# One program stretch for phase A, and a different order of its by-products

## The reference, cut to what matters

```python
x = x + jnp.tanh(g_xattn[0]) * _L0_xattn_ref(ctx_1024, _layernorm(x), mask, ...)   # 16 heads of 64, 512 keys
x = x + jnp.tanh(g_ffn[0]) * _L0_ffn_ref(_layernorm(x), ...)                       # 16 heads of 16, gated
x = x + jnp.tanh(g_xattn[1]) * _L1_xattn_ref(_layernorm(x), ctx_1024, ..., 16)     # 16 heads of 16
x = x + jnp.tanh(g_ffn[1]) * _L1_ffn_ref(_layernorm(x), ...)                       # 32 experts, best 1
...   # layers 2 and 3: an attention, a small net, an attention, 32 experts with the best 4
```

## Time and profile before

| what | us |
|---|---|
| median of 3 runs | 4738.97 (4735.92 to 4742.37) |
| profiled execution, own time | 4746.18 |
| its span | 4744.5 |
| PE busy | 4112.5 (87%) |
| DVE busy | 2320.8 (49%) |
| ACT busy | 1780.9 (38%) |
| POOL busy | 953.1 (20%) |

### The profile page before, as it was taken

How to read it: one execution, slowest core, us unless ns; L and a number is a source line. 1 busy time by engine, 2 the same in 40 slices (tenths; PEclk the granted TensorE clock), 3 DMA queues, 4 the chain that set the end, 5 groups by cost and what they waited for, 6 DMA issues and landing times. The chain is left out here.

```text
span 4744.5 us, 77442 instructions
## 1 busy us (share of the span) xinstructions
PE 4112.5 (87%) x29168; PEld 2852.5 (60%) x29168; DVE 2320.8 (49%) x7126; ACT 1780.9 (38%) x3733; POOL 953.1 (20%) x1113
## 2 busy tenths in 40 slices
PE   5999899989998999999996699996899899769986
PEld 3655655565556555655564359995566666438853
DVE  2545554555455545554543322212556666574335
ACT  3445444544554455445542111111343444313320
POOL 1212221222122212221211001111000010005557
PEclk9999999999999999999997799996899999879998
DMA  3000000000000000000000207991000000028974
GB/s 104 1 3 8 8 3 5 8 8 3 6 8 8 3 6 8 8 3 6 6 5 5 107 5 245 333 325 58 12 21 23 19 21 15 12 85 317 389 202 125
DMA packets 132637, 300.85 MB, mean 63 GB/s; under 512 B 19953, under 2 KB 86065, under 8 KB 123697
## 3 DMA queue, kind: packets, MB, share of 16 engines
q1 hardware_dynamic: 81968, 216.69, 12.8%
q0 software_dynamic: 18336, 50.09, 3.7%
q10 hardware_dynamic: 31968, 29.11, 1.8%
HBM read 245.76 MB, written 50.07 MB: 62 GB/s over the span
## 5 line engine op out<-in xcount | busy, mean ns | idle before, releaser
L487 POOL TENSOR_SCALAR a_wide_p<-a_wide_p,a_w_inv 128x512 f32<-128x512 f32 x512 | 362.7, 721 | 1553.1 <-DVE a_w_inv L1029 1552.1
L851 ACT ACTIVATE a_wide_p<-a_wide_p,a_row_min 128x512 f32<-128x512 f32 x512 | 364.1, 713 | 46.7 <-DVE a_row_min L1024 42.3
L1099 DVE TENSOR_REDUCE a_q_pad<-ring 128x4 f32<-128x1024 f32 x256 | 301.7, 1221 | 155.5 <-PE ring L679 151.7
L1024 DVE CUSTOM_DVE_ANT_0 a_wide_p<-ring,a_neg_keys 128x512 f32<-128x512 f32 x434 | 285.0, 687 | 108.9 <-PE ring L553 108.1
L553 PE MATMUL ring<-a_qk 64*128 64x512 f32 x868 | 291.7, 647 | 3.7 <-DVE a_wide_pt L1034 1.6
L899 ACT ACTIVATE a_probs<-ring 128x1024 f32<-128x1024 f32 x256 | 247.4, 1019 | 90.0 <-PE ring L693 90.0
L1446 PE MATMUL ring<-b_xgt,b_we 128*128 128x128 f32 x2016 | 235.9, 275 | 2.8 <-issue 2.3
L1446 PEld LDWEIGHTS ring<-b_xgt,b_we 128*128 128x128 f32 x2016 | 230.1, 192 | 4.1 <-issue 3.2
L2418 DVE CUSTOM_DVE_ANT_0 c_junk<-ring,c_neg_mask 128x256 f32<-128x256 f32 x512 | 182.6, 420 | 99.7 <-PE ring L1985 99.2
L583 PE MATMUL ring<-a_wide_pt,a_v 128*64 128x256 f32 x1792 | 219.8, 388 | 0.0
L679 PE MATMUL ring<-a_k_t,a_q_t 32*128 32x256 f32 x2048 | 154.2, 415 | 73.4 <-DVE a_q_pad L1099 48.9
(11 more groups left out here) (429 smaller groups left out, 8362.6 us busy)
## 6 DMA issues: line engine op xcount, KB each, us to landing
b_we<-in_experts SPq DMA_DIRECT2D x63, 1536.0 KB, 9.6
d_we<-in_experts SPq DMA_DIRECT2D x159, 384.0 KB, 6.2
d_results<-d_yb ACTq DMA_DIRECT2D x159, 128.0 KB, 6.1
b_results<-b_yb ACTq DMA_DIRECT2D x63, 128.0 KB, 9.3
x_all<-in_x SPq DMA_DIRECT2D x1, 4096.0 KB, 14.1
a_cb<-in_ctx SPq DMA_DIRECT2D x16, 256.0 KB, 2.7
b_turned<-a_heads_t SPq DMA_DIRECT2D x16, 256.0 KB, 2.4
b_rows<-a_heads SPq DMA_DIRECT2D x16, 256.0 KB, 2.1
```

The source lines that it names most:

```text
L487: ins = pool.tensor_scalar(wide_p[:, h % 4, t, :], wide_p[:, h % 4, t, :], w_inv[:, t, h:h + 1], 1.0, ALU.mult, ALU.mult)
L851: ins = act.activation(wide_p[:, h % 4, t, :], wide_p[:, h % 4, t, :], ACT.Exp, scale=-1.0, bias=row_min[:, h, t:t + 1], accum_out=row_sum ...
L1024: dve.tensor_tensor_reduce(wide_p[:, h % 4, t, :], wbank(name), neg_keys[w % 2][:], -0.125, 3.0e38, ALU.add, ALU.min, row_min[:, h, t:t + ...
L1099: dve.tensor_reduce(q_pad[:, :, 2 * i:2 * i + 2, HD].rearrange("p t h -> p h t"), s, AX.X, ALU.max, negate=True).then_inc(nr.taken(name), 1)
```

## The change

The two stretches ahead of the main one are gone, and their work stands at the head of the main one. SP issues, in this order: the first context, the first two tiles of `x`, `wkv`, `wq`, the mask, the two other contexts, the rest of `x`, and then the 21 remaining loads. ACT issues the temperature, the gates and the four norm columns. Each group has a semaphore of its own, on which its first reader waits. DVE waits for the remaining loads in `constants()`, ahead of step 2 of round 0.

In the loop, six things stand elsewhere:

- DVE's reciprocal of the second tile's sums, in steps 1, 4 and 6, stands ahead of the norms at the third place of the step, and POOL scales that tile ahead of two roots.
- In step 7, PE transposes the first tile of weights, and DVE copies it, ahead of a group by query and of its maxima.
- The fourth group by query stands later: that of f after the scores of t=1 in step 4, that of c in step 0 of the next round, after the first scores. The maxima follow.
- The counting of the routing moves from place 22 to 23, DVE's ranking after the l norm.
- ACT copies f's turned queries ahead of the exponentials of the second tile in step 3.
- ACT's narrow exponentials of one group stand between the two copies of weights, and its first copy of the summed values stands one place earlier, before the next wide exponentials.

```diff
-        with Stage() as ctx:
...
-                sp.dma_start(x_all[:], a["x"].rearrange("b (t p) d -> p (b t) d", p=P)).then_inc(loaded, 16)
-                sp.dma_start(gates[:, 0:4], every("g_xattn")).then_inc(loaded, 16)
-                sp.dma_start(gates[:, 4:8], every("g_ffn")).then_inc(loaded, 16)
-                sp.wait_ge(loaded, 48)
...
-                act.wait_ge(loaded, 48)
-                act.activation(gates[:], gates[:], ACT.Tanh).then_inc(gated, 1)
...
-                with Stage() as ctx:
...
-                    loads = [
-                        (wq[:], a["L0_xattn_Wq"].rearrange("(c p) n -> p c n", p=P)),
-                        (wkv[:], a["L0_xattn_Wkv"].rearrange("(c p) n -> p c n", p=P)),
-                        (wout[:], a["L0_xattn_Wout"].rearrange("(c p) n -> p c n", p=P)),
...
-                        (temp[:, 0, :], every("temperature_row")),
-                        (w1[:], a["w1_t"].rearrange("(c p) n -> p c n", p=P)),
...
-                    @block.sync
-                    def _(sp):
-                        for dst, src in loads:
-                            sp.dma_start(dst, src).then_inc(loaded, 16)
-                        sp.wait_ge(loaded, 16 * len(loads))
...
-                        dve.wait_ge(loaded, 16 * len(loads))
...
+                    loads = [
+                        (wout[:], a["L0_xattn_Wout"].rearrange("(c p) n -> p c n", p=P)),
+                        (ln_o[:, 0, :], every("L0_xattn_ln_o_g")), (ln_o[:, 1, :], every("L0_xattn_ln_o_b")),
...
+                        x = a["x"].rearrange("b (t p) d -> p (b t) d", p=P)
+                        context(0)
+                        sp.dma_start(x_all[:, 0:2, :], x[:, 0:2, :]).then_inc(first_loaded, 16)
+                        sp.dma_start(wkv[:], a["L0_xattn_Wkv"].rearrange("(c p) n -> p c n", p=P)).then_inc(wkv_loaded, 16)
+                        sp.dma_start(wq[:], a["L0_xattn_Wq"].rearrange("(c p) n -> p c n", p=P)).then_inc(wq_loaded, 16)
+                        sp.dma_start(mask_u8[:], every("mask_keys")).then_inc(mask_loaded, 16)
+                        for b in range(1, min(B, 3)):
                             context(b)
+                        sp.dma_start(x_all[:, 2:T, :], x[:, 2:T, :]).then_inc(latents_loaded, 16)
+                        for dst, src in loads:
+                            sp.dma_start(dst, src).then_inc(loaded, 16)
...
-                                if u == 1 and on(f):
-                                    root("o", o_norm, f + 1)
-                                if u == 6 and on(f):
-                                    root("c", c_norm, f + 1)
                                 if on(i):
                                     scale(i, u, 1)
                                 if u == 1 and on(f):
+                                    root("o", o_norm, f + 1)
                                     root("f", f_norm, f + 1)
+                                if u == 6 and on(f):
+                                    root("c", c_norm, f + 1)
...
                                     e_logits(c0)
-                                if p == 22:
+                                if p == 23:
                                     e_count(c0)
...
                                     queries("f", f)
-                                if 17 <= p <= 20:
+                                if 17 <= p <= 19:
                                     by_query("f", f, p - 17)
...
                                     queries("c", f)
-                                if 36 <= p <= 39:
+                                if 36 <= p <= 38:
                                     by_query("c", f, p - 36)
...
+                        pe.wait_ge(made, 2)
                         for i in range(-1, B + 2):
+                            if i == 1:
+                                pe.wait_ge(loaded, 16 * len(loads))
+                                pe.wait_ge(made, 10)
                             for u in range(PAIRS):
                                 nw, nu = pair_after(i, u)
                                 bw, bu = pair_before(i, u)
                                 if on(i):
                                     scores(i, u, 0)
+                                if u == 0 and on(i - 2):
+                                    by_query("c", i - 2, 3)
                                 if on(nw):
                                     keys(nw, nu)
                                 beside(i, 5 * u)
                                 if on(i):
                                     scores(i, u, 1)
+                                if u == 4 and on(i - 1):
+                                    by_query("f", i - 1, 3)
                                 if on(nw):
                                     pair_queries(nw, nu)
                                 beside(i, 5 * u + 1)
@@ -825,9 +784,12 @@
                                 beside(i, 5 * u + 2)
                                 if on(bw):
                                     pair_values(bw, bu)
+                                if u == PAIRS - 1 and on(i):
+                                    weights_by_key(i, u, 0)
                                 beside(i, 5 * u + 3)
+                                if u < PAIRS - 1 and on(i):
+                                    weights_by_key(i, u, 0)
                                 if on(i):
-                                    weights_by_key(i, u, 0)
                                     weights_by_key(i, u, 1)
                                 beside(i, 5 * u + 4)
...
-                                if p in (5, 6):
-                                    values_out("c", c0, p - 5)
-                                if 2 <= p <= 5:
-                                    narrow_exps("c", c0, p - 2)
+                                if p in (2, 4, 5):
+                                    narrow_exps("c", c0, (2 * p - 4, 2 * p - 3))
+                                if p in (4, 6):
+                                    values_out("c", c0, p // 2 - 2)
...
-                                if p == 16:
-                                    turn_queries(("f", "Q", f))
                                 if p == 22:
                                     nr.wait_full(act, ("f", "S", f, 7))
                                     turn_queries(("f", "Q2", f))
-                                if p in (26, 27):
-                                    values_out("f", f, p - 26)
-                                if 23 <= p <= 26:
-                                    narrow_exps("f", f, p - 23)
+                                if 24 <= p <= 26:
+                                    narrow_exps("f", f, (2 * p - 46, 2 * p - 45))
+                                if p in (25, 27):
+                                    values_out("f", f, (p - 25) // 2)
...
+                        act.dma_start(temp[:, 0, :], every("temperature_row")).then_inc(temp_loaded, 16)
+                        act.dma_start(gates[:, 0:4], every("g_xattn")).then_inc(gates_loaded, 16)
+                        act.dma_start(gates[:, 4:8], every("g_ffn")).then_inc(gates_loaded, 16)
+                        for i, n in enumerate(("ln_x_g_cols", "ln_x_b_cols", "ln_l_g_cols", "ln_l_b_cols")):
+                            act.dma_start(ln_cols[:, i, :], a[n]).then_inc(ln_loaded, 16)
+                        act.wait_ge(gates_loaded, 32)
+                        act.activation(gates[:], gates[:], ACT.Tanh).then_inc(gated, 1)
+                        act.wait_ge(stepped, 1)
+                        act.activation(temp[:, 2, :], temp[:, 1, :], ACT.Exp).then_inc(stepped, 1)
+                        act.wait_ge(stepped, 3)
+                        act.activation(temp[:, 4, :], temp[:, 3, :], ACT.Ln).then_inc(stepped, 1)
+                        act.wait_ge(ln_loaded, 64)
...
+                                if u == 3 and on(i - 1):
+                                    turn_queries(("f", "Q", i - 1))
...
-                                if on(i):
-                                    take_weights(i, u, 0)
-                                    take_weights(i, u, 1)
+                                for t in range(2):
+                                    if u == 0 and on(i - 2):
+                                        narrow_exps("c", i - 2, (2 + t,))
+                                    if u == 4 and on(i - 1):
+                                        narrow_exps("f", i - 1, (t,))
+                                    if on(i):
+                                        take_weights(i, u, t)
                                 beside(i, 5 * u + 4)
...
+                                if p == 0:
+                                    maxima("c", c0, 3)
...
-                                if 17 <= p <= 20:
+                                if 17 <= p <= 19:
                                     maxima("f", f, p - 17)
+                                if p == 21:
+                                    maxima("f", f, 3)
...
+                        def constants():
```

(19 more changed lines are left out.)

156 lines of the change are left out of this document (76 added, 80 removed).

## The result

| kernel | median us | runs |
|---|---|---|
| before | 4737.44 (4729.70 to 4742.37) | 4 |
| after | 4538.99 (4537.02 to 4539.24) | 4 |

The ratio is 0.9576, 95% interval 0.9562 to 0.9589: 198.5 us less. The forecast was 168.3 us less, 4570.7 us. The time lies in the wide range, 4530 to 4620, but outside the inner one of 4548 to 4600, and it is nearer to the rival "more than forecast" (4524 us) than to the forecast itself. The profiled execution of after took 4539.24 us, its span is 4537.5, against 4744.5 before: 207.0 us.

The account below looks back on a forecast made before the run. Loads and waits for them bound the opening, PE the loop. Opening 36.9, rounds 2 to 15 123.2, round 1 6.0 and round 16 2.2 sum to 168.3 us off 4738.97: 4570.7 us, range 4530 to 4620, inner 4548 to 4600.

Parts of the forecast that it names:

- more than forecast: Rival: in the rounds the waits vanish with little behind them, 12 us a round; 4524 us, chance 0.08.
- The opening: Before the loop: first scores 38.7 us earlier once the mask row's loads land at 14.9; less 1.8 for constants, 36.9 us.
- The gates: In the opening: at best landed in 3 us at no cost, at worst at 15.6, costing 7.2 us; the first was taken.
- Step 1: In a round: POOL's wait of 1.74 us goes, the rest turns into a wait for DVE; gain 0.4 us.
- the named wait for DVE's copy: Sign: PE's scores of step 2 wait for DVE's copy of weights, once a round, over 1 us.
- The walk of the full round: Gains at each wait of a full round, summing to 9.4 us; 8.8 after a deduction, a round of 148.7.
- steps 3 to 5: In a round, with f's attention: five waits go, sum 5.7 us, 0.6 let come back; gain 5.1 us.
- step 6: In a round: POOL's scaling wait of 1.74 us goes, ACT's copies follow PE by 0.2; gain 1.5 us.
- the further deduction of 0.6 for hops: Taken off the round's 9.4 us for engine-to-engine latency left out where a wait nearly closes; leaves 8.8 us.
- c's part: Step 7 to step 1, c's attention: group and row-minimum waits 1.0 us, earlier copy of summed values 1.42; gain 2.4 us.
- the other terms: Outside the 13 full rounds: opening 36.9 us, first interval 6.0, last interval 8.8, last mark to end 2.2.
- the 147 to 151 named as a sign: Sign in the loop: the wide output product should recur every 147 to 151 us in the changed kernel's profile.

Follow-up runs that it names:

- e1: before without its two opening stretches, with the loads of after (old loop behind new opening): 4703.8 us, 0.9925 of before.
- e8: after with the mask loaded ahead of wkv, norm columns ahead of the gates on ACT's queue, DVE's wait for ACT's exponential behind the first norms: 4542.4 us.
- e6: after with step 7's transposes and copy of the first tile of weights behind the wide output again: 4557.0 us.
- e10: before with only DVE's reciprocal ahead of the norms in steps 1, 4 and 6 and POOL's scaling ahead of its roots: 4697.4 us.
- e3: after with DVE's second-tile reciprocal behind the norms again in steps 1, 4 and 6, POOL's roots ahead of its scaling: 4582.8 us.
- e11: after with SP loading norm columns and mask ahead of wkv, DVE's wait for ACT's exponential behind first norms, ln_o's bias added in step 0: 4522.85 us.

## Why the prediction was right, and where it was short

*The opening*: right in its chain, 38.5 by the marks, 37.1 by e1, for 36.9. What ended the chain is the one named, the mask row, at 16.17 us instead of 14.9. The norm columns, which the working didn't price, were there at 15.8, 1.3 us ahead of the latents' transposes. The first scores start at 24.86 for 24.2, a gain of 38.0 instead of 38.7. `constants()` stood at 47.59 us without a wait, between 45 and 50, and made PE wait for 0.67 us (at 50.96) where 1.8 were taken off; there are 18 loads behind it, not 21, and they were there by 40.5 us instead of 43.8. The size is in part luck: in before the granted clock is 0.55 from 72.7 to 76.5 us, in step 0, in after 1.00 at that place, which is 1.2 us that the forecast knew nothing of.

*The gates*: priced at no cost by choice, with 7.2 us as the other bound. No row stood behind the 3 us of the lower bound; here they took 3.9 and 5.2 us and landed at 5.1 and 6.9 us, which costs nothing, as DVE then stood for 3.45 us for the mask. The rule of the Trainium skill that the prediction cites, "DMA: Bandwidth & Descriptors", section on queues, rings and completion order, has the transfer engines take turns between queues. The gates agree with it; the columns issued from 2.2 us on do so only in part, as 1 KB took 8.8 to 11.8 us beside SP's stream. e8 shows that the other bound was real: gates of 2 KB behind four small transfers came at 15.9 us, where the bound had 15.6. So the choice was right by luck: it hung on the gates standing ahead of the columns in ACT's queue, which the prediction had not used as an argument.

*Step 1*: the mechanism is right, and the named wait for DVE's copy stands there with 0.92 us, for "over 1 us". DVE's work from c's heads to the copy is 5.96 us instead of 6.77. The gain is 0.83 for 0.4, as DVE's and POOL's contention went too (0.72 us of DVE's time).

*The walk of the full round* gave 9.4, and 10.60 was measured against the round that was walked. It had 11.6 us of waits that go and 2.1 that come back (1.3 in step 1, 0.6 in steps 3 to 5, 0.2 in step 6). In the two traces 12.5 us of PE's waits go and 2.3 come back: 0.92 for DVE's copy, and 0.3 each for ACT's `a_kv_t` in step 6, for its copy of weights where the row minimum stood, and twice for exponentials. So what came back was already in the walk, and the further deduction of 0.6 for hops was the first step that failed. The second lies in *c's part*, 2.94 for 2.4: of its three waits for maxima, 0.55, 0.65 and 0.60 us, only one of 0.55 is left, where the walk took 0.2 off the last alone. The row for the maxima is the one that the earlier trace rows leaves out; the 15.6 us of idle time are not all in its six rows. That e6's edit carries half of c's gain, 1.46 us a round, the forecast did not see; it priced the group's move as if the copy of weights stayed early by itself.

*Half clock* is the third, by omission: 0.77 us a round, and with the longer idle time of the other rounds 1.05. The working took one round of 157.51 us, the second shortest, for all. The range of intervals, 157.5 to 159.6, was there to be read, and e10 shows that the sums' edit alone ends it.

In sum: 13 full rounds gave 150.8 - 114.4 = 36.4 us more than forecast; the other terms together 2.3. By the medians the shortfall is 30.2, as 8.5 us of the 207.0 are the profiled executions' own. The rounds, of 146.9 us, lie just under the 147 to 151 named as a sign, and they gained nearly the 12 us of the rival "more than forecast". As it has it, the waits vanish with little behind them (12.5 us against 2.3); 0.77 of the 11.6 us is the clock, which it doesn't name.

## What to carry to other kernels

Read more than one round, and compare their lengths before taking one for all: where a loop does the same work each time and its rounds have two lengths, the difference is not in its list; here it was mostly the clock behind a wait. Where an edit moves work away from in front of an instruction, look at every bank that this instruction needs: a copy that was early enough becomes late, and the edit that repairs it costs 3 us when tried in the old order and is worth 20 us beside the other. And where an engine works without a gap before a wait, changing the order renames the wait; taking something out of the stretch shortens it.

## What the runs showed that was not expected

- A product of 1.89 us took up to 3.55 (clock 0.52) behind a wait of 1.99 us for POOL, in 5 of the 13 full rounds of before and again in e1 and e3; once in before the fall came behind a wait of 1.60. In the eleven kernels where these waits are gone, no full round is longer by such a step.
- DVE's two-input operations took 689 and 632 ns beside POOL's scaling, and 480 and 482 without it; in e3, where they meet again, one group has 808 on average.
- Transfers of 1 and 2 KB from ACT's queue landed 3.5 to 5.2 us after their issue when issued by 1.8 us, and 7.3 to 12.1 us after it when issued from 2.2 us on, beside SP's megabytes (after, e8 and e11). In e11 the four columns, issued by SP ahead of the mask and `wkv`, landed in 3.2 to 3.6 us each. In all three the quick ones were those issued ahead of SP's large transfers, from either queue; no run separates this order from the moment of issue.
